# Part of VectorE's elementwise work between the stages of a graph network kernel goes to GpSimd, and its mask instructions are fused

## The reference

```
def hyp_linear(x, W, b, c):
    res = proj(mobius_matvec(W, x, c), c)
    hyp_b = proj(expmap0(b.reshape(1, -1), c), c)
    return proj(mobius_add(res, hyp_b, c), c)

def hyp_agg(x, src, dst, w, c, n_nodes):
    xt = logmap0(x, c)
    msg = xt[src] * w[:, None]
    agg = jax.ops.segment_sum(msg, dst, num_segments=n_nodes)
    return proj(expmap0(agg, c), c)

def mobius_add(x, y, c):
    x2, y2, xy = row sums of x*x, y*y, x*y
    num = (1.0 + 2.0 * c * xy + c * y2) * x + (1.0 - c * x2) * y
    den = 1.0 + 2.0 * c * xy + c * c * x2 * y2
    return num / jnp.clip(den, MIN_NORM)
```

## Time and profile before

| what | value |
|---|---|
| time, median of 3 runs | 1174.49 us (1174.16 to 1177.11) |
| the profiled execution's own time | 1179.44 us |
| its span, first to last instruction | 1177.6 us |
| mean granted TensorE clock | 0.947 of full speed |
| busy: PE, PEld | 1032.8 us (88%), 953.7 us (81%) |
| busy: DVE, ACT, POOL | 1044.3 us (89%), 716.7 us (61%), 698.6 us (59%) |

### The profile page before, as it was taken

One profiled execution on the slowest core, in us unless ns is written; L12 is line 12 of the kernel. 1 busy time (PEld: TensorE's weight loads), 2 busy tenths in 40 slices (PEclk: granted clock), 3 DMA queues, 4 the chain that ended last, 5 costly groups with the idle time before them and its releaser, 6 DMA issues.

```text
span 1177.6 us, 53896 instructions
## 1 busy us (share of the span) xinstructions
PE 1032.8 (88%) x21722; PEld 953.7 (81%) x21722; DVE 1044.3 (89%) x1393; ACT 716.7 (61%) x1977; POOL 698.6 (59%) x334
## 2 busy tenths in 40 slices
PE   3079999999999999637997699999999999999998
PEld 2058888888888888637997579999999999999997
DVE  8879999999999999684664798999999999999995
ACT  5348988888888888510002565555556556556663
POOL 7005788888888888100000356777777777777774
PEclk9569999999999999759998789999999999999999
DMA  2002323222222222678950444444444444444450
GB/s 82 0 34 97 127 102 121 107 115 107 115 111 112 111 112 113 257 298 321 409 210 31 148 125 159 157 158 155 159 162 161 158 152 158 156 160 162 162 162 29
DMA packets 44878, 169.98 MB, mean 144 GB/s; under 512 B 19441, under 2 KB 19767, under 8 KB 44828
## 3 DMA queue, kind: packets, MB, share of 16 engines
q1 hardware_dynamic: 44827, 169.28, 39.9%
HBM read 121.11 MB, written 48.14 MB: 144 GB/s over the span
## 4 chain that ended last, share of the span: by engine, by line
PE 62%; DVE 17%; ACT 12%; issue 6%; POOL 1%; DVEq 1%; ACTq 0%; POOLq 0%
PE PS L1617 18%; PE PS L1619 12%; ACT arena L694 8%; PE PS L1632 8%; PE PS L1487 8%; PE PS L1470 5%; PE PS L1637 3%; DVE arena L1106 3%; PE PS L1449 3%; DVE arena L1083 2%; DVE arena L1091 2%; DVE arena L1069 1%; DVE arena L1078 1%; PE PS L1518 1%; DVE rows L884 1%
## 5 line engine op out<-in xcount | busy, mean ns | idle before, releaser
L625 POOL TENSOR_TENSOR arena<-arena 128x512 bf16<-128x512 f32 x240 | 342.0, 1442 | 142.0 <-ACT arena L821 142.0
L598 POOL TENSOR_TENSOR aggTw<-aggTw,arena 128x72 f32 x48 | 318.3, 6631 | 133.4 <-ACT arena L705 133.4
L1617 PE MATMUL PS<-arena 125*128 125x128 bf16 x3600 | 344.1, 219 | 1.4 <-DVE HTw L1316 0.3
L821 ACT ACTIVATE arena<-arena 128x512 bf16<-128x512 f32 x240 | 150.7, 628 | 186.3 <-DVE arena L1333 186.3
L1617 PEld LDWEIGHTS PS<-arena 125*128 125x128 bf16 x3600 | 250.1, 97 | 7.9 <-issue 5.3
L694 ACT ACTIVATE arena<-arena 128x72 bf16<-128x72 bf16 x864 | 217.2, 341 | 4.2 <-DVE arena L1091 2.0
L1487 PE MATMUL PS<-arena,A 125*64 125x72 f32 x4800 | 180.6, 231 | 25.5 <-DVE A L987 21.7
L1487 PEld LDWEIGHTS PS<-arena,A 125*64 125x64 f32 x4800 | 166.0, 139 | 32.4 <-issue 24.3
L1333 DVE SCALAR_TENSOR_TENSOR arena<-PS,arena 128x512 f32<-128x512 f32 x240 | 159.4, 680 | 28.7 <-ACT arena L828 28.7
L828 ACT ACTIVATE arena<-PS 128x512 bf16<-128x512 f32 (+2 forms) x336 | 171.7, 545 | 2.2 <-PE PS L1619 2.1
L1619 PE MATMUL PS<-arena 108*128 108x128 bf16 x1200 | 167.2, 220 | 0.0
(11 more groups left out here) (199 smaller groups left out, 1493.4 us busy)
## 6 DMA issues: line engine op xcount, KB each, us to landing
adjacency<-arena SPq DMA_DIRECT2D x48, 900.0 KB, 3.7
arena<-adjacency SPq DMA_DIRECT2D x46, 900.0 KB, 7.8
Bw<-slot_rows SPq DMA_DIRECT2D x48, 800.0 KB, 4.1
Cw<-slot_rows SPq DMA_DIRECT2D x48, 700.0 KB, 4.4
arena<-q_table SPq DMA_DIRECT2D x144, 18.0 KB
q_table<-arena SPq DMA_DIRECT2D x6, 336.0 KB
slot_rows<-slot_row SPq DMA_DIRECT2D x49, 13.0 KB
x_sb<-in_x SPq DMA_DIRECT2D x1, 700.0 KB
```

The source lines that it names most:

```text
L598: nc.gpsimd.tensor_tensor(win, win, taken[k], ALU.add).then_inc(added, 1)
L625: nc.gpsimd.tensor_tensor(H3[k][:, at_b, 2, :], Hs[k][:, 4 * q:4 * q + 4, :], H3[k][:, at_b, 1, :], ALU.subtract).then_inc(s_low_set, 1)
L821: nc.scalar.activation(H3[k][:, at_b, 1, :], Hs[k][:, 4 * q:4 * q + 4, :], ACT.Copy).then_inc(s_mid_set, 1)
L1617: mm(ps, OTs[k][:, b, :], P3[:, b, part, :], start=(part == 0), stop=False)
```

## The change

- ScalarE copies MU into A, both pieces, ahead of the squares (`mu_copied`), and the squares are asked for earlier: once y stands in the first layer, at the start of `act_scales(0)` in the second.
- GpSimd multiplies that copy by y into C (`products`), in both layers, and VectorE doesn't any more.
- GpSimd, once AC and BC stand (`vector_rows`), forms the second piece (nine blocks, 576 columns) of `AC * mx + BC * y` in three instructions (`second_piece`); VectorE multiplies it by ATN in one. VectorE waits for it ahead of AC * ATN. The first piece stays with VectorE as it was.
- GpSimd forms field 4 of `fieldT` in two halves, and the loop waits for them.
- GpSimd's memset of `aggTw` stands behind the first layer's products and second piece; its eight memsets of stage 3 stand behind `products(1)` and ahead of `second_piece(1)`.
- VectorE's instructions behind AC and BC: clamp, clip and 1 - NX become `scalar_tensor_tensor`s; the polynomial's first product is folded into the next by scaling the coefficients; each mask is fused with its product. Three instructions fewer a layer.

The rest of the diff declares the semaphores `mu_copied`, `pool_products`, `vector_rows`, `pool_steps`, and leaves out a few that were not used.

```diff
@@ -258,6 +258,8 @@
         p_stored, q3_set, q_stored = sem("p_stored"), sem("q3_set"), sem("q_stored")
         self_ps, self_set = sem("self_ps"), sem("self_set")
         squares_read = sem("squares_read")
+        mu_copied, pool_products, vector_rows = sem("mu_copied"), sem("pool_products"), sem("vector_rows")
+        pool_steps = sem("pool_steps")
         relu_squared = sem("relu_squared")
         fin_ps, fin_set, out_stored = sem("fin_ps"), sem("fin_set"), sem("out_stored")
         q_tail = sem("q_tail")
@@ -570,6 +572,35 @@
             for s in loop_sems:
                 pool.sem_inc(s, PRIMED)
             pool.sem_inc(primed, 1)
+            pool.wait_ge(w_second, 1)
+            for a in range(0, TILES, TILES // 2):
+                cols = slice(a, a + TILES // 2)
+                pool.tensor_tensor(fieldT[:, cols, 4, :], u[3][:, cols].unsqueeze(2).broadcast_to([128, TILES // 2, 2]),
+                                   fieldT[:, cols, 3, :], ALU.subtract).then_inc(fields_set, 1)
+
+            def wide(r, b):
+                return rows[0:PN, r, b].unsqueeze(2).broadcast_to([PN, b.stop - b.start, F])
+
+            def products(l):
+                y = yb[0:PN, l, :].unsqueeze(1)
+                pool.wait_ge(vector_rows, 1 + l)
+                for i, b in enumerate(PIECES):
+                    pool.wait_ge(mu_copied, 2 * l + i + 1)
+                    pool.tensor_tensor(C[:, b, :], A[:, b, :], y.broadcast_to([PN, b.stop - b.start, F]), ALU.mult)\
+                        .then_inc(pool_products, 1)
+
+            def second_piece(l):
+                b = PIECES[1]
+                y = yb[0:PN, l, :].unsqueeze(1)
+                pool.wait_ge(vector_rows, 2 + l)
+                pool.tensor_tensor(A[:, b, :], A[:, b, :], wide(10, b), ALU.mult).then_inc(pool_steps, 1)
+                pool.tensor_tensor(C[:, b, :], y.broadcast_to([PN, b.stop - b.start, F]), wide(11, b), ALU.mult)\
+                    .then_inc(pool_steps, 1)
+                pool.wait_ge(pool_steps, 2 * l + 2)
+                pool.tensor_tensor(A[:, b, :], A[:, b, :], C[:, b, :], ALU.add).then_inc(pool_products, 1)
+
+            products(0)
+            second_piece(0)
             pool.memset(aggTw[:, :], 0.0).then_inc(agg_cleared, 1)
 
             def any_gather(i, table, dest):
@@ -604,6 +635,7 @@
             fast = in_order(pool, 1)
             for l in range(2):
                 if l == 1:
+                    products(1)
                     with pool.If(fast == 1):
                         pool.wait_ge(ht_set, len(QUADS))
                         pool.wait_ge(sq_set, len(QUADS))
@@ -611,6 +643,8 @@
                         for table in (degree, aggTw):
                             for a in range(0, NW, CLEAR):
                                 pool.memset(table[:, a:min(a + CLEAR, NW)], 0.0).then_inc(agg_cleared, 1)
+                if l == 1:
+                    second_piece(1)
                 with pool.If(fast == 0):
                     pool.wait_ge(xt_stored, 16 * (l + 1))
                     any_gather(l, xt_d, G)
@@ -746,6 +780,8 @@
             answer_tanh()
             for l in range(2):
                 sc.wait_ge(mu_ps, l + 1)
+                for b in PIECES:
+                    nc.scalar.activation(A[:, b, :], MU[:, b, :], ACT.Copy).then_inc(mu_copied, 1)
                 for b in PIECES:
                     square(B[:, b, :], MU[:, b, :])
                 answer_tanh()
@@ -927,17 +963,12 @@
                 y = yb[P_, l, :].unsqueeze(1).broadcast_to([PN, NB, F])
                 y2 = y2s[P_, l:l + 1]
                 tt(row(T), row(S), row(S), ALU.mult)
-                ve.wait_ge(mu_ps, l + 1)
-                ask_square()
-                tt(C[:, PIECES[1], :], MU[:, PIECES[1], :], y[:, PIECES[1], :], ALU.mult)
-                ask_square()
-                squares_ready(1)
-                tt(C[:, PIECES[0], :], MU[:, PIECES[0], :], y[:, PIECES[0], :], ALU.mult)
                 squares_ready()
                 link(ve.tensor_reduce(row(Q_), B[:, :, :], X, ALU.add))
 
                 tt(row(T2), row(T), row(Q_), ALU.mult)
                 post(ve.tensor_scalar(a_, row(T2), MIN_NORM, None, ALU.max))
+                ve.wait_ge(pool_products, 3 * l + 2)
                 link(ve.tensor_reduce(row(Z), C[:, :, :], X, ALU.add))
                 take()
                 link(ve.reciprocal(row(T1), s_))
@@ -955,6 +986,7 @@
                 link(ve.scalar_tensor_tensor(row(AC), row(T3), y2, row(T), ALU.add, ALU.mult))
                 ts(row(BC), row(SS), -1.0, ALU.mult, 1.0, ALU.add)
                 tt(both(AC), both(AC), each(T1), ALU.mult)
+                ve.sem_inc(vector_rows, 1)
 
                 tt(both(T1), both(AC), both(Q_), ALU.mult)
                 link(ve.scalar_tensor_tensor(row(T1), row(T2), 2.0, row(T1), ALU.mult, ALU.add))
@@ -962,30 +994,30 @@
                 tt(row(T2), row(BC), row(BC), ALU.mult)
                 link(ve.scalar_tensor_tensor(row(T2), row(T2), y2, row(T1), ALU.mult, ALU.add))
 
-                ask(ve.tensor_scalar(a_, row(T2), MIN_NORM, None, ALU.max))
-                ts(row(NX), s_, MAXNORM, ALU.min)
-                ts(row(T2), row(NX), -1.0, ALU.mult, 1.0, ALU.add)
+                ask(ve.scalar_tensor_tensor(a_, row(T2), MIN_NORM, row(T2), ALU.max, ALU.max))
+                link(ve.scalar_tensor_tensor(row(NX), s_, MAXNORM, s_, ALU.min, ALU.min))
+                link(ve.scalar_tensor_tensor(row(T2), row(NX), -1.0, ones[P_, 0:NB], ALU.mult, ALU.add))
                 link(ve.reciprocal(row(T2), row(T2)))
                 link(ve.reciprocal(row(T1), s_))
                 post(ve.scalar_tensor_tensor(a_, row(NX), 1.0, row(T2), ALU.add, ALU.mult))
                 tt(row(T3), row(NX), row(NX), ALU.mult)
-                ts(row(ATN), row(T3), ARTANH[0], ALU.mult)
-                for c in ARTANH[1:]:
-                    link(ve.scalar_tensor_tensor(row(ATN), row(ATN), c, row(T3), ALU.add, ALU.mult))
-                link(ve.scalar_tensor_tensor(row(ATN), row(ATN), 1.0, row(NX), ALU.add, ALU.mult))
-                ts(row(T2), row(NX), SMALL, ALU.is_lt)
-                tt(row(ATN), row(ATN), row(T2), ALU.mult)
-                ts(row(T2), row(NX), SMALL, ALU.is_ge, 0.5, ALU.mult)
+                lead = ARTANH[0]
+                link(ve.scalar_tensor_tensor(row(ATN), row(T3), ARTANH[1] / lead, row(T3), ALU.add, ALU.mult))
+                for c in ARTANH[2:]:
+                    link(ve.scalar_tensor_tensor(row(ATN), row(ATN), c / lead, row(T3), ALU.add, ALU.mult))
+                link(ve.scalar_tensor_tensor(row(ATN), row(ATN), 1.0 / lead, row(NX), ALU.add, ALU.mult))
+                link(ve.scalar_tensor_tensor(row(ATN), row(NX), SMALL, row(ATN), ALU.is_lt, ALU.mult))
                 take()
-                tt(row(T2), row(T2), s_, ALU.mult)
-                tt(row(ATN), row(ATN), row(T2), ALU.add)
-                tt(row(ATN), row(ATN), row(T1), ALU.mult)
+                link(ve.scalar_tensor_tensor(row(T2), row(NX), SMALL, s_, ALU.is_ge, ALU.mult))
+                link(ve.scalar_tensor_tensor(row(ATN), row(T2), 0.5 / lead, row(ATN), ALU.mult, ALU.add))
+                link(ve.scalar_tensor_tensor(row(ATN), row(ATN), lead, row(T1), ALU.mult, ALU.mult))
+                ve.wait_ge(pool_products, 3 * l + 3)
                 tt(both(AC), both(AC), each(ATN), ALU.mult)
-                for b in PIECES:
-                    tt(A[:, b, :], MU[:, b, :], wide(row(AC), b), ALU.mult)
-                    tt(C[:, b, :], y[:, b, :], wide(row(BC), b), ALU.mult)
-                    ve.tensor_tensor(A[:, b, :], A[:, b, :], C[:, b, :], ALU.add).then_inc(xt_set, 1)
-
+                first, second = PIECES
+                tt(A[:, first, :], MU[:, first, :], wide(row(AC), first), ALU.mult)
+                tt(C[:, first, :], y[:, first, :], wide(row(BC), first), ALU.mult)
+                ve.tensor_tensor(A[:, first, :], A[:, first, :], C[:, first, :], ALU.add).then_inc(xt_set, 1)
+                ve.tensor_tensor(A[:, second, :], A[:, second, :], wide(row(ATN), second), ALU.mult).then_inc(xt_set, 1)
 
             ve.wait_ge(consts_set, 5)
             ve.tensor_copy(ramp[:, :], rampi[:, :])
@@ -1029,8 +1061,6 @@
             squares_ready()
             link(ve.tensor_reduce(row(SS), C[:, :, :], X, ALU.add))
             clamp_scale(row(S), row(SS))
-            ve.wait_ge(w_second, 1)
-            tt(fieldT[:, :, 4, :], twice(u[3]), fieldT[:, :, 3, :], ALU.subtract)
             ve.wait_ge(base_ps, 2)
             link(ve.tensor_scalar(flag[:, 1:2], PS[:, 3072:3073], float(E), None, ALU.is_equal))
             link(ve.tensor_copy(oki[0:1, 0:1], flag[0:1, 1:2]))
@@ -1044,11 +1074,14 @@
             link(ve.tensor_reduce(rows[P_, Q_, 0:2], ysq[P_, :, :], X, ALU.add))
             tanh_scale(row(T), row(NX), row(Q_))
             tt(yb[P_, :, :], yb[P_, :, :], rows[P_, T, 0:2].unsqueeze(2).broadcast_to([PN, 2, F]), ALU.mult)
+            ve.sem_inc(vector_rows, 1)
```

(12 more changed lines are left out.)

## The result

The changed kernel takes 1181.8 us (median of 7 runs, 1178.77 to 1184.57), the one before 1174.49 (1172.14 to 1177.11). The ratio is 1.0054, 95% interval 1.0035 to 1.0074: slower by 6.3 us, 4.1 to 8.7. The forecast was 1177.4, so +2.9.

A forecast was written before the change was run, and what follows sets the result against it. Bound mostly by TensorE (62% of the chain), but by VectorE's short instructions in the two touched stretches. First layer -0.7 and second +3.55 gave +2.9 us on the 1174.49 median: 1177.4 us, range 1170.3 to 1181.0.

The forecast's parts named there:

- own line of 3.5 us: The difference from the kernel before at which the measurement tells a change from none: 0.3%, 3.5 us.
- A reading under parts 1 to 4: VectorE and GpSimd hold each other up: one waits for a whole instruction of the other, even for short ones.
- Part 1: Weights' third part, first stretch: GpSimd takes VectorE's 1700-column subtraction, a tensor_scalar is held; gain 1.3 us, bounds 0.5 and 1.96.
- Part 2: Products by y go to GpSimd, holding T = S*S in the first layer; gain 0.7 us there, 0.66 in the second.
- Part 3: Second layer's memsets moved behind the products: tensor_scalars each wait for the running memset; 1.5 us lost, bounds 0 and 3.0.
- the walk: Second layer's chain stepped against the memset train: four tensor_scalars lose about 0.3, 0.7, 0.4 and 0.1, 1.5 us lost.
- Rival (c): Second layer's memsets cost all five tensor_scalars 0.61 us: 3.0 instead of 1.5, sum +4.4, 1178.9 us; chance 0.25.
- Part 4: Nine blocks on GpSimd behind AC and BC: 3.5 us lost a layer, 1.58 gained in the first, 0.19 in the second.
- Rival (a): Short instructions behind AC and BC slip through beside GpSimd, no stall: sum -4.1, 1170.4 us, faster; chance 0.17.
- (b): Behind AC and BC GpSimd is the one held: 2.9 us lost a layer, sum +1.7, 1176.2 us; chance 0.10.
- Part 5: Masks fused behind AC and BC: three instructions fewer a layer, 0.65 us gained in each.

The follow-up runs named there:

- gaps: Changed kernel with GpSimd waiting for each of the eight memsets before issuing the next; touched stretches +2.7 us against the kernel before, one run.
- nosecond: Changed kernel with VectorE forming the nine blocks again, GpSimd keeping the products by y and weights' part; ratio 1.0032 to the kernel before.
- alone: Changed kernel with VectorE waiting for the clamp to complete before issuing the row sum; touched stretches +6.7 us against the kernel before, one run.
- late_after: Changed kernel with four more reciprocals (1.4 us) ahead of the second layer's clamp; touched stretches +6.2 us against the kernel before, one run.
- best_asks: Changed kernel, nine blocks on VectorE, five tensor_scalars given second SBUF inputs, first-layer yb*yb, S*S before GpSimd's release, squares requested before tanh; ratio 0.9962 to kernel before.

## Why the prediction was right and wrong

**The direction and most of the mechanism.** The forecast was a small loss out of two engines holding each other up, and that is what is there. The size was off: +2.9 us forecast, +6.3 measured. The upper end of the range, 1181.0, is just over the 1180.8 that the ratio gives, and under the 1181.8 of the seven runs' own median. That the range held is luck: it was built from a memset loss of at most 3.0 us, which came out at 5.0, and from stalls at 4.1 a layer, which came out at 2.9. By the prediction's own line of 3.5 us the result is "slower", to which it gave 0.37, less than the 0.49 for "same".

**A reading under parts 1 to 4 was too wide.** "So one waits for a whole instruction of the other" is not what the row at 14.87 us shows. That `tensor_scalar` is over at 15.77, while GpSimd's L564 beside it is listed to 17.20, and in the same L564 the 1024-column instruction of L922, with two SBUF inputs, runs from 16.40 in its usual 1.22 us. L564 is a `tensor_scalar` of GpSimd's. Beside GpSimd's `tensor_tensor`s, which is what the change adds, the reading held in the changed kernel: the instructions at 28.98, 36.59 and 38.88 end within 0.15 us of the GpSimd instruction beside them.

**Part 1** was right: y stands at 35.51 instead of 36.70, 1.2 us won (1.3 forecast), and the `tensor_scalar` is held as described.

**Part 2, first layer, failed in its size.** It was to add 0.7 to part 1's 1.3; L967 came only 0.5 us earlier in all, so 0.7 of part 1 was lost instead. The step read "VectorE's 25-column T = S*S falls due at 36.4, beside it, and is held". It overlooked yb*yb ahead of it, also with two SBUF inputs, and took the semaphore increments in front of it (the release of GpSimd and two requests for squares) as nothing: yb*yb starts 0.75 us later behind y than before, 0.51 of it between the two requests, and so falls behind the start of L589 at 36.03. So two instructions were held, by both pieces (1.93 and 0.94 us). In the second layer L967 won 0.88 us (0.66 forecast).

**Part 3 is the step that failed.** "Each waits for the memset that runs: 0 to 0.73, on average 0.36 ... 1.5 us lost." One `tensor_scalar` waited for all eight, 5.2 us more than its own time, of which 5.0 came out on the chain; even the upper bound was 3.0. The bound came from one row of the kernel before, in which a train opened at a memset's end. With the waits of `gaps` the walk's total comes out, 1.5 us, though not its four parts (0.24, 0.38, 0.55 and 0.33 for 0.3, 0.7, 0.4 and 0.1); without them, behind the products, it doesn't. Rival (c) had the right place and the wrong mechanism: not five short waits but one long one.

**Part 4** was right in kind and 0.6 us a layer too high: 2.9 lost (3.84 for 0.91), 3.5 forecast. VectorE's first instruction did not get in ahead of GpSimd, as forecast: GpSimd's stands at 47.20, VectorE's at 47.22. GpSimd's products of 576 columns took 1.15 us, not 1.28, and its sum 1.44 with a wait. Rival (a) falls: of the four short instructions three took 1.05 to 1.27 us. So does (b): GpSimd was not kept out. The increments took 0.15, not 0.05.

**Part 5** was right, and a gain of 0.4 us was not foreseen: the pause of 0.41 us ahead of the first aggregation vanished.

**Measured, by the same steps.** First layer: -0.51 (parts 1 and 2) + 0.15 + 2.93 - 0.65 - 1.58 - 0.4 = -0.1 (read: -0.02). Second layer: -0.88 + 5.0 + 0.15 + 2.93 - 0.65 = +6.55 (read: 6.56); the 0.19 that TensorE waited for the second piece went as well, but lies behind the point that is read.

## What to carry to other kernels

Work that is handed from VectorE to GpSimd is not out of VectorE's way: price each product or sum of GpSimd's (a `tensor_tensor` out of SBUF) at its full length on every VectorE instruction with two SBUF inputs beside it, even one of 25 columns, and look for VectorE work with one SBUF input that is no `tensor_scalar` to put there (the row sum took 1.82 us beside GpSimd's products, as without them). Don't let a `tensor_scalar` on the critical chain fall due beside GpSimd memsets that stand behind its products without a wait: give it a second SBUF input (0.19 us instead of 5.36), or put a wait between the memsets. The handover that was kept in the kernels that gained, the products by y, ran beside ScalarE's squares and VectorE's row sum; the nine blocks, put beside two-input instructions, cost more than they saved.

## What the runs showed of the hardware that was not expected

- A 25-column `tensor_scalar` of one operation waited for all that was left of a train of memsets behind GpSimd's products: 5.36, 5.37 and 3.97 us, and 3.98 for the rest of a subtraction and one memset. One of two operations, in trains of memsets alone, was let in at the next end: 0.79, 0.44, 0.82 us. Whether the train or the form of the `tensor_scalar` tells the two apart was not tested.
- A row sum issued behind the held `tensor_scalar` ended with it (503.11 + 5.27), while alone behind it it needed 1.82 us more: it had run during the wait.
- Two semaphore increments in VectorE's program took 0.5 us between them in one place (behind y); moved ahead of the tanh, the pair added 0.23 us of idle time there.
- The stretch from the first aggregation's start to `arg<-PS` took either 437.3 us (before, changed, nosecond, alone, gaps, late_after, best_asks) or 435.0 to 435.6 (the other seven), in kernels that are alike there. A difference of two profiled spans up to 2.3 us says nothing by itself. The cause is open.
